# Latent attention: maxima behind the score halves issued 3, 2, 2, 1 instead of 2, 2, 2, 2; one of two roundings of q on VectorE

## The reference

```python
def _L0_xattn_ref(x, latents, Wq, Wkv, Wo, ln1_w, ln1_b, ln2_w, ln2_b):
    xn = _layernorm(x, ln1_w, ln1_b)
    ln = _layernorm(latents, ln2_w, ln2_b)
    q = ln @ Wq
    kv = jnp.concatenate([xn, ln], axis=-2) @ Wkv
    k, v = jnp.split(kv, 2, axis=-1)
    q, k, v = (heads(q), heads(k), heads(v))
    scale = 1.0 / np.sqrt(np.sqrt(DIM_HEAD))
    logits = jnp.einsum('bhld,bhsd->bhls', q * scale, k * scale)
    w = jax.nn.softmax(logits.astype(jnp.float32), axis=-1).astype(logits.dtype)
    out = jnp.einsum('bhls,bhsd->bhld', w, v)
    return out.transpose(0, 2, 1, 3).reshape(B, L, INNER) @ Wo

x = x + _L0_xattn_ref(ctx_1024, _layernorm(x, axis=-1), ...)
```

## Time and profile before

| | us |
|---|---|
| median of 3 runs | 4197.21 |
| lowest and highest | 4196.6, 4197.85 |
| the profiled execution | 4190.63 |
| its span | 4188.6 |
| stage A's units, first scores of unit 0 to first scores of unit 15 | 140.85 to 1116.3 |

### The profile page before, as it was taken

How to read it: one execution, slowest core, us unless ns; L and a number is a source line. 1 busy time by engine, 2 the same in 40 slices (tenths; PEclk the granted TensorE clock), 3 DMA queues, 4 the chain that set the end, 5 groups by cost and what they waited for, 6 DMA issues and landing times. The chain is left out here.

```text
span 4188.6 us, 40949 instructions
## 1 busy us (share of the span) xinstructions
PE 3057.8 (73%) x14046; PEld 1793.9 (43%) x14046; DVE 2086.7 (50%) x3654; ACT 1488.5 (36%) x2034; POOL 1038.2 (25%) x625
## 2 busy tenths in 40 slices
PE   4999999999956585497585888888289510079769
PEld 1555555545436353496352333332279400034344
DVE  3655655556314263375464677674267453721270
ACT  2344444444424233264232344445156210022230
POOL 0355656556621130301131000000400212001110
PEclk7899999999967797698697899998589755579899
DMA  2000000000004100463100000000156225000260
GB/s 86 4 6 2 4 5 5 5 1 4 2 26 154 41 1 15 159 220 132 30 1 10 3 1 5 4 0 2 55 206 217 67 23 59 3 23 31 86 236 20
DMA packets 92591, 204.64 MB, mean 49 GB/s; under 512 B 31145, under 2 KB 65577, under 8 KB 83738
## 3 DMA queue, kind: packets, MB, share of 16 engines
q0 software_dynamic: 18512, 109.48, 7.7%
q1 hardware_dynamic: 70458, 87.07, 7.7%
q10 hardware_dynamic: 3472, 6.16, 0.4%
HBM read 154.41 MB, written 48.01 MB: 48 GB/s over the span
## 5 line engine op out<-in xcount | busy, mean ns | idle before, releaser
L596 POOL TENSOR_TENSOR A_key_sums<-A_key_sums,A_probs 128x1024 f32<-128x1024 f32 (+1 forms) x224 | 526.9, 2371 | 227.7 <-ACT A_probs L489 227.7
L489 ACT ACTIVATE A_probs<-A_banks 128x512 f32<-128x512 f32 (+1 forms) x576 | 329.8, 597 | 386.4 <-PE A_banks L409 384.2
L539 DVE TENSOR_REDUCE A_part_max<-A_banks 128x1 f32<-128x367 f32 x768 | 354.0, 531 | 156.8 <-PE A_banks L330 155.5
L1656 ACT ACTIVATE F_probs<-F_banks 128x1024 f32<-128x1024 f32 x256 | 250.0, 1022 | 316.7 <-PE F_banks L1601 298.7
L1712 DVE TENSOR_REDUCE F_part_max<-F_banks 128x1 f32<-128x512 f32 x512 | 318.1, 683 | 30.5 <-PE F_banks L1556 28.9
L358 PE MATMUL A_banks<-A_probs,A_v_tok 128*64 128x512 f32 x1152 | 278.7, 605 | 0.0
L407 PE MATMUL A_banks<-A_q_one,A_k_one 128*128 128x512 f32 (+1 forms) x576 | 257.0, 446 | 26.3 <-ACT A_probs L489 23.3
L330 PE MATMUL A_banks<-A_k_one,A_q_one 128*128 128x368 f32 x768 | 230.2, 383 | 6.8 <-ACT A_v_tok L469 6.4
L2022 PE MATMUL G_banks<-G_path,G_ctx_rows 77*128 77x512 f32 x16 | 14.0, 1071 | 294.2 <-DMA G_ctx_rows<-in_G_ctx_rows 294.2
L409 PE MATMUL A_banks<-A_q_two,A_k_two 128*128 128x512 f32 (+1 forms) x576 | 228.0, 396 | 0.0
L1556 PE MATMUL F_banks<-F_k_split,F_q_split 64*128 64x512 f32 x512 | 195.1, 502 | 43.5 <-DVE F_part_max L1712 30.8
(11 more groups left out here) (531 smaller groups left out, 6406.6 us busy)
## 6 DMA issues: line engine op xcount, KB each, us to landing
H_w<-in_H_w SPq DMA_DIRECT2D x16, 1024.0 KB, 7.6
moe_in<-A_zeros ACTq DMA_DIRECT2D x1, 5888.0 KB, 17.4
D_tile_in<-moe_in SPq DMA_DIRECT2D x23, 256.0 KB, 5.3
moe_out<-D_z SPq DMA_DIRECT2D x23, 256.0 KB, 4.9
F_tile_in<-moe_in SPq DMA_DIRECT2D x23, 256.0 KB, 5.3
moe_out<-F_z SPq DMA_DIRECT2D x23, 256.0 KB, 4.9
slots<-H_staged SPq DMA_DIRECT2D x8, 512.0 KB, 3.5
made<-H_made POOLq DMA_DIRECT2D x16, 256.0 KB, 6.8
```

Source lines behind the costliest of these rows:

```text
L489: act.activation(probs[0:kw, j, kt % RING, blk * BLK:(blk + 1) * BLK], ps[0:kw, half % 3, :], ACT.Exp, scale=1.0 / 8.0).then_inc(s["exp_re ...
L539: dve.tensor_reduce(part_max[:, i // 3, i % 3:i % 3 + 1], ps[:, MAX_BANKS[i % 3], 0:PIECE], AX.X, ALU.max).then_inc(s["piece_max"], 1)
L596: pool.tensor_tensor(key_sums[0:kw, j, :], before, probs[0:kw, j, kt % RING, :], ALU.add).then_inc(s["summed"], 1)
L1656: act.activation(probs[:, i % RING, heads_at, :], ps[:, heads_at, :], ACT.Exp, scale=DH ** -0.5).then_inc(s["exp_ready"], 1)
```

## The change

It does two things. In key tiles 3 to 8 the eight pieces of maxima are issued 3, 2, 2 and 1 behind the four halves, where it was 2 behind each. And ScalarE rounds q for the first head only; VectorE rounds it for the second, with a copy from the banks, ahead of its two subtractions. The first subtraction waits for ScalarE's rounding, the second for VectorE's own.

```diff
+    MAXIMA_BEHIND = (3, 2, 2, 1)
...
-        names = """zeroed in_loaded out_loaded q_ps q_hi q_dup ...
+        names = """zeroed in_loaded out_loaded q_ps q_hi q_hi_other q_dup ...
...
-                            more()
-                            more()
+                            for _ in range(MAXIMA_BEHIND[2 * j + blk]):
+                                more()
...
             def q_hi(m, b):
                 act.wait_ge(s["q_ps"], m + 1)
-                for j in range(2):
-                    act.activation(q_one[OWN[j], b, j, :], bank_pair(6)[OWN[j]], ACT.Copy).then_inc(s["q_hi"], 1)
+                act.activation(q_one[OWN[0], b, 0, :], bank_pair(6)[OWN[0]], ACT.Copy).then_inc(s["q_hi"], 1)
...
             def split_q(m, b):
 
+                dve.wait_ge(s["q_ps"], m + 1)
+                dve.tensor_copy(q_one[OWN[1], b, 1, :], bank_pair(6)[OWN[1]]).then_inc(s["q_hi_other"], 1)
                 for j in range(2):
-                    dve.wait_ge(s["q_hi"], 2 * m + j + 1)
+                    dve.wait_ge(s[("q_hi", "q_hi_other")[j]], m + 1)
                     dve.tensor_tensor(q_two[OWN[j], b, j, :], bank_pair(6)[OWN[j]], q_one[OWN[j], b, j, :].bitcast(F32),
                                       ALU.subtract).then_inc(s["q_lo"], 1)
```

More of the change, by code:

```diff
@@ L221, in latent_attention @@
         ps = sc.psum()
-        names = """zeroed in_loaded out_loaded q_ps q_hi q_dup q_lo k_ps k_hi k_lo v_ps v_ready ctx_ps ctx_hi ctx_lo ctx_v
+        names = """zeroed in_loaded out_loaded q_ps q_hi q_hi_other q_dup q_lo k_ps k_hi k_lo v_ps v_ready ctx_ps ctx_hi ctx_lo ctx_v
                    k_second piece_ps piece_max nmax_ready rows_ps rows_ready row_ready score_ps exp_ready
```

## The result

| | before | after |
|---|---|---|
| median, us | 4196.91 (6 runs, 4192.85 to 4201.48) | 4220.63 (6 runs, 4219.57 to 4223.77) |
| the profiled execution, us | 4190.63 | 4221.34 |
| its span, us | 4188.6 | 4219.5 |
| ratio of the times | | 1.0058, 95% interval 1.0045 to 1.0071 |

The change makes the kernel 24 us slower. The prediction said slower, by 15.4; the measured time lies 1.6 us above its range.

A forecast was written before the change was run, and what follows sets the result against it. TensorE's own order was taken to bound the kernel at full clock. 13.5 us for the order of pieces plus 1.9 for the rounding gave 15.4 on the median 4197.2, so 4212.6 us, range 4201 to 4219.

The forecast's parts named there:

- The release law: Key tiles: each piece's weight load waits for the maximum three pieces earlier; VectorE spaces maxima 0.447 us whatever the order.
- part 1: Order 3, 2, 2, 1 in key tiles 4 to 8: values start 0.18 us later, 75 tiles, 13.5 us slower.
- list of signs: Expected in the trace: tiles 4 to 8 5.74 apart, tile 3 unchanged, three load waits a tile, longest about 0.4 us.
- Part 2: VectorE's rounding of q, around q: 1.9 us slower in sum, with ends of -1.0 and 1.9.
- the chain: Around q: copy, subtractions, output projection, addition to x, second projection in sequence; first projection starts 0.19 us later.
- the -1.0: Unit 0, which has no output projection: its stall of 1.37 us shrinks by 1.02, counted as -1.0.
- the 0.19: Around q: first output projection starts 0.19 us later in units 1 to 14, 2.7 us; prologue 0.2.
- (a): Rival, no difference: VectorE's spacing in the tiles falls to 0.36 when fed ahead; +1.9, 4199 us; chance 0.05.
- (b): Rival, faster: queued maxima in the tiles overlap freely, values start 0.19 sooner; -12, 4185 us; chance 0.06.
- (c): Rival, slower still: around q, copy and ScalarE's rounding take turns at shared banks; 15 us on top, 4228; chance 0.04.
- (d): Rival: ScalarE's rounding limited the stretch around q, its 1.02 us is won in every unit; -15, 4195; chance 0.05.

The follow-up runs named there:

- half-width runs: Maxima over 183 of 367 columns on the kernel before: 4161.73 us, 0.9921 with order 2, 2, 2, 2; 4163.59 us, 0.9929 with 3, 2, 2, 1.
- 3, 1, 2, 2: Kernel before with the pieces of maxima issued 3, 1, 2 and 2 behind the four halves: 4194.22 us, 0.9995.
- the run with late projections and ScalarE's roundings: Kernel before with the first output projection behind the eighth half and the second behind the values of key tile 0: 4190.31 us, 0.9994.
- three filled kernels with this order: Changed kernel with unused matmuls in the stop ahead of the first output projection: four, 4213.88 us; two, 4210.93 us; four again, 4213.55 us.
- second measurement: The changed kernel, unaltered, timed once more beside one with four extra matmuls: 4218.69 us, 1.0052 on the kernel before.

## Why the prediction was wrong

**What bounds.** Right as to the places: the loss is in TensorE's stream, at the loads of pieces and in the stretch around q. But the prediction counted only what lengthens TensorE's order, and a third of the loss is the same order run at a lower clock.

**The release law and part 1.** Right. 0.18 a tile was forecast, and 5.735 - 5.548 = 0.187 measured over 75 tiles; 13.5 us against 14.0, and the order alone measured 14. Key tile 3 was said to be unchanged; it is (6.17, 6.18). The waits of the loads came out smaller than its list of signs says: 0.27, 0.26 and 0.20 us, the longest not 0.4. That VectorE's spacing is what costs is shown by the half-width runs, and that it is the wait in front of the last half by 3, 1, 2, 2.

**Part 2, the chain.** Right in its steps up to the start of the projection. The copy takes 1.23 (1.22 taken), the subtractions start 1.26 after it, the stretch is 10.15 in place of 9.94, so 0.21 (0.19) in 14 units, 2.9 us. One size was off: the sixth half starts 6.54 us behind its unit's first scores where it was 7.73, so 1.19 sooner and not 1.02. For the same reason unit 0's stretch is 4.3 where runs with two roundings by ScalarE have 5.5, the -1.0 with 0.2 more, and the new stop is 1.50 and not 1.3. The table in the Trainium skill, "VectorE: DVE Perf Modes", section "The perf-mode tier table", allows a copy from PSUM up to the doubled rate. This copy does not get it: 1.23 is what a subtraction of the same size takes (1.22), the single rate that the page's section "Why PSUM operands drop a tier" gives for float32. The hold that its section "Two Vector instructions with no wait between them" describes for instructions in different quadrants agrees: 1.26 from start to start for a copy of 1.23.

**The step that failed** is the last one of part 2, that the 0.19 is handed on and is all. The prediction has the new stop (about 1.3 us, in its last part), but only asks when the next matmul starts, not how fast it then runs: it put the clock behind that stop at nothing, without a reason. The work behind it ran at 1.2 GHz for a part in seven of 14 units, at 1.0 to 1.7 us each, 8.8 us in the profiled execution and 10.7 in the second one. With them the loss from unit 0 to unit 15 adds up: 14.0 for the tiles, 2.9 for the later subtractions, 8.8 for the drops less 1.2 for the one drop of the kernel before, -1.2 in unit 0's stall, and 1.6 in key tile 0 of unit 0. That is 24.9, where the traces differ by 25.0. The 1.6 is not the change's: in this execution the clock rose later in unit 0 (granted 0.64 from 140 to 150 us, against 0.81), and the run with late projections and ScalarE's roundings, whose code for unit 0 is that of the kernel before, has it too (8.28 us for that tile, 6.74 before). Without the 8.8 the sum is 16.1. The traces of the three filled kernels with this order are 16.0 to 16.3 longer than the kernel before, and their times are 16 to 20 above it. The prediction speaks of a change of the clock only for later stages. That the second measurement's median fell inside the range is luck: its trace has eight drops.

The trace of the kernel before had a hint that I did not follow. Its unit 1 takes 11.15 us from key tile 1 to 2, where the others take 9.94: one drop of the same kind in 14 units. The granted clock there, and in the same stretch of unit 2:

```profile
211.00:214.50 3.50, 3.30 (x6) 1.43 (x6) 0.20 (x2) 0.80 (x2) 2.34 (x1) 0.64 0.00 0
277.30:280.80 3.50, 3.11 (x9) 1.43 (x8) 1.42 (x2) 1.59 (x4) 2.38 (x1) 1.00 0.00 0
```

Where the clock falls now and then already, a change that lengthens the stop should be priced with the fall. A count of units whose stretch is longer than the common one would have shown it.

**The rivals.** (a) and (b) fall: VectorE's spacing did not change, 3.66 for eight. (c) falls: the two engines read the same banks at once at their own rates, 1.02 and 1.23. (d) falls: the 1.02 is won only in unit 0.

**What stays open.** What in the stops the clock answers to. In all traces, every drop of units 1 to 14 begins 8.9 to 9.8 us behind the unit's first scores. So of the stops around q only the two ahead of that point can have brought it, and not the one of 0.39 ahead of the second projection, which ends at 11.9 or later. The longer of the two grew only from 1.39 to 1.50 and their sum from 1.50 (1.39 and 0.11) to 1.71 (0.21 and 1.50), while the drops went from 4 in 70 to 18 in 42. Both filling and moving shorten both. The version with late projections and ScalarE's roundings has one stop of 1.38 and no drop in 14 units, which is no contradiction to 4 in 70. Nor do these two figures say which unit drops, since all units of a kernel have nearly the same stops. It is not settled either why the rounding alone had three drops and the whole change seven and eight: the units' length differs (65.38 and 66.30 us), no run varied it alone, and the trace of the rounding alone is of an execution 11.6 us below its median.

## What to carry to other kernels

Where two engines pass banks in a short ring, work out each release time from the consumer's spacing and put the producer's other work in front of the releases, the last of it above all; issuing more at the front does not help if the consumer never rests. A wait that goes away is a gain only if the next thing in the queue isn't waiting for something later: here 1.2 us less of one wait became 1.4 more of the next, and only work moved ahead of that next wait turned the rounding on VectorE into a gain. Price the clock with the stop: look how often the same stretch already runs slow in the kernel before.

## What the runs showed of the hardware

- Behind stops of 0.21 and 1.50 us, 0.7 us apart, the granted clock fell from 2.4 to 1.2 GHz in 18 of 42 units, and each fall cost 1.0 to 1.7 us. With the longer stop filled down to 0.59 (42 units) or 1.05 (14 units) there was no fall.
- Four matmuls that nobody uses, put into that stop, made the kernel 5 us faster in the median of the same rounds.
- VectorE's maxima of 367 columns come every 0.447 us although each lasts 0.53, while the copy and the two subtractions of 1024 columns, each of which begins on other partitions than the one in front, come 1.25 to 1.26 apart and last 1.22 to 1.23.
- ScalarE's rounding and VectorE's copy read the same two banks at the same time, each on its own 64 partitions, and take 1.02 and 1.23 us, as long as ScalarE's alone (1.02) and a copy from banks alone (1.22).
